# Flamingo block: the first layer's weight preparation moved into its attention, loads in pieces

## The reference

```python
x = x + tanh(g_xattn[0]) * L0_xattn(layernorm(x), ctx_1024, Wq, Wk, Wv, Wo, gq, gk)

q = (h @ Wq).reshape(B, Sq, H, D)
k = (ctx @ Wk).reshape(B, Skv, H, D)
v = (ctx @ Wv).reshape(B, Skv, H, D)
q, k = rmsnorm(q, gq), rmsnorm(k, gk)
attn = softmax(einsum("bqhd,bkhd->bhqk", q, k) / sqrt(D))
out = einsum("bhqk,bkhd->bqhd", attn, v).reshape(B, Sq, H * D)
return out @ Wo
```

## Time and profile before

| | us |
|---|---|
| median of three runs | 1361.18 |
| lowest and highest | 1357.79, 1362.24 |
| profiled execution | 1358.81 |
| its span, first to last instruction | 1357.0 |
| PE busy (share of the span) | 1271.7 (94%) |
| DVE, ACT, POOL busy | 903.0, 775.1, 435.9 |

### The profile page before, as it was taken

How to read it: one execution, slowest core, us unless ns; L and a number is a source line. 1 busy time by engine, 2 the same in 40 slices (tenths; PEclk the granted TensorE clock), 3 DMA queues, 4 the chain that set the end, 5 groups by cost and what they waited for, 6 DMA issues and landing times. The chain is left out here.

```text
span 1357.0 us, 23635 instructions
## 1 busy us (share of the span) xinstructions
PE 1271.7 (94%) x8163; PEld 1126.9 (83%) x8163; DVE 903.0 (67%) x2515; ACT 775.1 (57%) x2112; POOL 435.9 (32%) x420
## 2 busy tenths in 40 slices
PE   3799999999999969999999987999999999998998
PEld 3588888888888858888888875899898988887987
DVE  4688888888987657743433344667676677786867
ACT  3577777777777714322222255666666666545552
POOL 1365556654665523200000001222124242252430
PEclk8899999999999969999999998999999999999999
DMA  7000000000000400210000020000000003413435
GB/s 255 9 1 2 9 1 0 0 8 0 0 0 1 99 1 1 84 41 1 0 0 1 1 70 16 1 9 1 1 17 25 1 32 129 114 63 91 127 93 183
DMA packets 44237, 50.50 MB, mean 37 GB/s; under 512 B 14345, under 2 KB 36370, under 8 KB 43378
## 3 DMA queue, kind: packets, MB, share of 16 engines
q1 hardware_dynamic: 40354, 38.92, 9.7%
q0 software_dynamic: 3792, 10.40, 2.1%
HBM read 36.82 MB, written 12.49 MB: 36 GB/s over the span
## 5 line engine op out<-in xcount | busy, mean ns | idle before, releaser
L955 POOL TENSOR_TENSOR probs_a<-probs_a,rden_a 128x512 f32<-128x512 f32 x128 | 133.2, 1041 | 337.5 <-DVE rden_a L914 337.5
L98 PE MATMUL bank<-wvo_hi,pc_hi_a 128*128 128x256 f32 x512 | 154.0, 301 | 1.9 <-DVE pc_lo_a L921 1.9
L1321 ACT ACTIVATE act_g_f<-bank 128x512 f32<-128x512 f32 x64 | 38.2, 597 | 189.2 <-PE bank L100 189.2
L99 PE MATMUL bank<-wvo_lo,pc_hi_a 128*128 128x256 f32 x512 | 144.2, 282 | 0.0
L100 PE MATMUL bank<-wvo_hi,pc_lo_a 128*128 128x256 f32 x512 | 144.2, 282 | 0.0
L1378 DVE TENSOR_TENSOR hid_f<-act_g_f,bank 128x512 f32<-128x512 f32 x64 | 44.0, 688 | 143.3 <-ACT act_g_f L1321 143.3
L826 ACT ACTIVATE pc_hi_a<-bank 128x512 fp32r<-128x512 f32 x128 | 76.6, 598 | 107.3 <-PE bank L100 105.4
L917 DVE TENSOR_TENSOR pt_lo_a<-bank,pt_hi_a 128x512 fp32r<-128x512 f32 x128 | 87.8, 686 | 58.9 <-ACT pt_hi_a L823 58.3
L817 ACT ACTIVATE probs_a<-bank,nbias_a,q_r_a 128x128 f32<-128x128 f32 x256 | 114.4, 474 | 21.5 <-DVE nbias_a L908 21.5
L921 DVE TENSOR_TENSOR pc_lo_a<-bank,pc_hi_a 128x512 fp32r<-128x512 f32 x128 | 88.1, 688 | 45.3 <-ACT pc_hi_a L826 45.3
L98 PE MATMUL bank<-xt_hi_f,w_gu_hi_f 128*128 128x512 f32 (+1 forms) x256 | 102.0, 399 | 0.0
(11 more groups left out here) (304 smaller groups left out, 3989.9 us busy)
## 6 DMA issues: line engine op xcount, KB each, us to landing
xs_raw_f<-rows_in SPq DMA_DIRECT2D x39, 129.0 KB
q_raw_p<-in_L_xattn_Wq SPq DMA_DIRECT2D x4, 1024.0 KB, 8.5
y_tok_f<-rows_out SPq DMA_DIRECT2D x4, 1024.0 KB, 9.6
we_raw<-in_L_ffn_We_gate_up SPq DMA_DIRECT2D x2, 1408.0 KB, 10.8
o_raw_p<-in_L_xattn_Wo SPq DMA_DIRECT2D x1, 2048.0 KB, 10.2
x_sb<-in_x SPq DMA_DIRECT2D x4, 512.0 KB, 13.8
ctx_raw_a<-in_ctx SPq DMA_DIRECT2D x8, 256.0 KB, 2.8
o_early<-in_L_xattn_Wo SPq DMA_DIRECT2D x1, 2048.0 KB, 15.0
```

The lines of the kernel that those rows point to most:

```text
L98: nc.tensor.matmul(out, w[0], x[0], start=start, stop=False)
L99: nc.tensor.matmul(out, w[0], x[1], start=False, stop=False)
L955: nc.gpsimd.tensor_tensor(probs[:, i % 2, :, :], probs[:, i % 2, :, :], scale, ALU.mult).then_inc(sem("probs_scaled"), 1)
```

## The change

For layer 0 the preparation block is gone (what is left serves layer 1 only and is renamed `prepare_second`). Its work becomes steps of the attention's own order:

- SP issues context of group 0, then a quarter of Wk (256 KB), the tokens of group 0, a quarter of Wq (512 KB), the two gain vectors, the second quarters, Wv, Wo, the other quarters, the other tokens and the gates' vectors.
- WK and WQ split one quarter each: the high part on ACT, the low part on DVE for quarters 0 and 1, on POOL for 2 and 3. VT, VTc are the transposes of Wv and their copies; VO, VOc the products of two heads and their split. VT and VO take part in the ring of two banks.
- VT 0 and 1 lie ahead of Q0 in the start part, VT 2 and 3 behind the first scores. Two VO fills go into the start quad and into each of the quads 1, 2 and 3, behind Kc3 and KTc3 (in quad 3 behind Qq2 and KTc3). Quarter 2 of both weights is split in the start quad, quarter 3 in quad 1.
- K, Q and W wait for their pieces. The first group's four quads are written out (part "first"), and the loop runs over two groups in place of three. In the start part Qv2 and Qv3 wait for QT0 and QT1.
- The raw matrices now lie in the space of the low parts (Wk, Wq, Wo) and of `wvo_hi` (Wv and its transposes). The tanh of the gates and the product of the gains move to VOc7 and KN0.

```diff
-                    sp.dma_start(small[:, 0:2], a["g_xattn"].partition_broadcast(P)).then_inc(loaded_s, 16)
-                    sp.dma_start(small[:, 2:4], a["g_ffn"].partition_broadcast(P)).then_inc(loaded_s, 16)
-                    sp.dma_start(small[:, 4:5], a["L0_xattn_gq"].rearrange("(p a) -> p a", a=1)).then_inc(loaded_s, 16)
-                    sp.dma_start(small[:, 5:6], a["L0_xattn_gk"].rearrange("(p a) -> p a", a=1)).then_inc(loaded_s, 16)
-                    sp.dma_start(v_raw[:, :], Wv).then_inc(loaded_v, 16)
-                    sp.dma_start(o_raw[:, :, :], Wo.rearrange("(h d) e -> d h e", d=P)).then_inc(loaded_o, 16)
                 for k in range(KD):
                     sp.dma_start(q_raw[:, k, :], Wq[k * P:(k + 1) * P]).then_inc(loaded_q[k], 16)
-                if layer == 0:
-                    sp.dma_start(k_raw[:, :], Wk).then_inc(loaded_k, 16)
-                if layer == 0:
-                    for g in range(G):
-                        tokens = slice(g * GB, (g + 1) * GB)
-                        sp.dma_start(core.x[:, tokens, :], a["x"][tokens].rearrange("b s d -> s b d")).then_inc(core.x_loaded[g > 0], 16)
...
-                    pool.wait_ge(raw_hi, 2)
-                    nc.gpsimd.tensor_tensor(w["q"][1][:, 1, :], q_raw[:, 1, :], f32(w["q"][0][:, 1, :]), ALU.subtract)
...
-                        nc.scalar.activation(w["q"][0][:, k, :], q_raw[:, k, :], ACT.Copy).then_inc(raw_hi, 1)
...
-                    act.wait_ge(loaded_k, 16)
-                    nc.scalar.activation(w["k"][0][:, :], k_raw[:, :], ACT.Copy).then_inc(raw_hi, 1)
...
-                        nc.vector.tensor_tensor(w["q"][1][:, 0, :], q_raw[:, 0, :], f32(w["q"][0][:, 0, :]), ALU.subtract)
...
-                    dve.wait_ge(raw_hi, KD + 1)
-                    nc.vector.tensor_tensor(w["k"][1][:, :], k_raw[:, :], f32(w["k"][0][:, :]), ALU.subtract)
...
+    start = listed("""
+        WK0 CT0 CT1 LNA0 K0 Kc0 K1 Kc1 Kq0 LNB0 Kr0 K2 Kc2 Kq1 Kr1 K3 Kc3 Kq2 Kr2 WQ0 X0 X1 Kq3 Kr3 KN0 KH0 KH1 KH2 KH3 WK1 WQ1 VT0 VTc0 VT1 VTc1
+        Q0 Qv0 Qq0 Q1 Qv1 Qq1 Qr0 Qp0 Q2 QT0 QTc0 Qv2 Qq2 Qr1 Qp1 Q3 QT1 QTc1 Qv3 Qq3 Qr2 Qp2 QT2 QTc2 Qr3 Qp3 QT3 QTc3
+        KT0 KTc0 KT1 KTc1 KT2 KTc2 KT3 KTc3""")
+    start += [("S", 0, NQ), ("Sm", 0, NQ), ("CN", 0, pre)] + listed("VT2 VTc2 VT3 VTc3")
+    start += with_weights([s for s in quad_order(NQ) if s[0] not in ("W", "E")], {"Kc3": "VO0", "Tl0": "VOc0", "KTc3": "VO1", "QTc3": "VOc1", "Rp2": "WK2", "KH3": "WQ2"})
     body = [s for j in range(1, NQ + 1) for s in quad_order(j)]
+    first = with_weights(quad_order(1), {"Kc3": "VO2", "Tl0": "VOc2", "KTc3": "VO3", "QTc3": "VOc3", "Rp2": "WK3", "KH3": "WQ3"})
+    first += with_weights(quad_order(2), {"Kc3": "VO4", "Tl0": "VOc4", "KTc3": "VO5", "QTc3": "VOc5"}) + with_weights(quad_order(3), {"Qq2": "VO6", "Th2": "VOc6", "KTc3": "VO7", "QTc3": "VOc7"}) + quad_order(NQ)
...
+                for s in orders["first"]:
+                    emit("first", 0, *s)
+                with emit.engine.Fori(1, G - 1) as g:
...
+            if L == 0:
+                def columns(t):
+                    return slice(t * QH * P, (t + 1) * QH * P)
+                def tokens(m):
+                    own = slice(m * GB, (m + 1) * GB)
+                    sp.dma_start(core.x[:, own, :], a["x"][own].rearrange("b s d -> s b d")).then_inc(core.x_loaded[m > 0], 16)
+                def keys_of(t):
+                    sp.dma_start(w["k_raw"][:, columns(t)], a["L0_xattn_Wk"][:, columns(t)]).then_inc(sem(f"wk_loaded{t}"), 16)
+                def queries_of(t):
+                    sp.dma_start(w["q_raw"][:, :, columns(t)], a["L0_xattn_Wq"].rearrange("(k p) n -> p k n", p=P)[:, :, columns(t)]).then_inc(sem(f"wq_loaded{t}"), 16)
+                keys_of(0)
+                tokens(0)
+                queries_of(0)
+                sp.dma_start(small[:, 4:5], a["L0_xattn_gq"].rearrange("(p a) -> p a", a=1)).then_inc(sem("gains_loaded"), 16)
+                sp.dma_start(small[:, 5:6], a["L0_xattn_gk"].rearrange("(p a) -> p a", a=1)).then_inc(sem("gains_loaded"), 16)
+                keys_of(1)
+                queries_of(1)
+                sp.dma_start(w["v_raw"][:, :], a["L0_xattn_Wv"]).then_inc(sem("wv_loaded"), 16)
+                sp.dma_start(w["o_raw"][:, :, :], a["L0_xattn_Wo"].rearrange("(h d) e -> d h e", d=P)).then_inc(sem("wo_loaded"), 16)
+                for t in range(2, NQ):
+                    keys_of(t)
+                    queries_of(t)
+                for m in range(1, G):
+                    tokens(m)
+                sp.dma_start(small[:, 0:2], a["g_xattn"].partition_broadcast(P)).then_inc(sem("small_loaded"), 16)
+                sp.dma_start(small[:, 2:4], a["g_ffn"].partition_broadcast(P)).then_inc(sem("small_loaded"), 16)
...
+                elif name == "VT":
+                    if i == 0:
+                        pe.wait_ge(sem("wv_loaded"), 16)
+                    for a_ in range(4):
+                        last = nc.tensor.transpose(bank[:, a_ * P:(a_ + 1) * P], w["v_raw"][:, (4 * i + a_) * P:(4 * i + a_ + 1) * P], core.ident[:, :])
+                elif name == "VO":
+                    if i == 0:
+                        pe.wait_ge(sem("wo_loaded"), 16)
+                        pe.wait_ge(sem("vt_copied"), 4)
+                    for h in (2 * i, 2 * i + 1):
+                        last = nc.tensor.matmul(bank[:, h % 2 * D:(h % 2 + 1) * D], w["v_t"][:, h, :], w["o_raw"][:, h, :], start=True, stop=True)
...
+                        pe.wait_ge(sem("wk_split"), t + 1)
...
+                        if L == 0:
+                            pe.wait_ge(sem("wq_split"), (j + 1) % NQ + 1)
...
+                    if L == 0 and i % 2 == 0:
+                        pe.wait_ge(sem("vo_split"), (j - 1) * 2 + i // 2 + 1)
...
+                elif name == "WK":
+                    act.wait_ge(sem(f"wk_loaded{i}"), 16)
+                    cols = slice(i * QH * P, (i + 1) * QH * P)
+                    nc.scalar.activation(w["k"][0][:, cols], w["k_raw"][:, cols], ACT.Copy).then_inc(sem("wk_hi"), 1)
+                elif name == "WQ":
+                    act.wait_ge(sem(f"wq_loaded{i}"), 16)
+                    cols = slice(i * QH * P, (i + 1) * QH * P)
+                    nc.scalar.activation(w["q"][0][:, :, cols], w["q_raw"][:, :, cols], ACT.Copy).then_inc(sem("wq_hi"), 1)
+                elif name == "VTc":
+                    nc.scalar.activation(flat(w["v_t"][:, 4 * i:4 * i + 4, :]), bank[:, :], ACT.Copy).then_inc(sem("vt_copied"), 1)
+                elif name == "VOc":
+                    nc.scalar.activation(flat(w["vo"][0][:, 2 * i:2 * i + 2, :]), bank[:, :], ACT.Copy).then_inc(sem("vo_hi"), 1)
+                    if i == 7:
+                        act.wait_ge(sem("small_loaded"), 32)
+                        nc.scalar.activation(core.gates[:, :], small[:, 0:4], ACT.Tanh).then_inc(sem("gates_made"), 1)
...
+                elif name == "WK" and i < 2:
+                    dve.wait_ge(sem("wk_hi"), i + 1)
+                    cols = slice(i * QH * P, (i + 1) * QH * P)
+                    nc.vector.tensor_tensor(w["k"][1][:, cols], w["k_raw"][:, cols], f32(w["k"][0][:, cols]), ALU.subtract).then_inc(sem("wk_split"), 1)
+                elif name == "WQ" and i < 2:
+                    dve.wait_ge(sem("wq_hi"), i + 1)
+                    cols = slice(i * QH * P, (i + 1) * QH * P)
+                    nc.vector.tensor_tensor(w["q"][1][:, :, cols], w["q_raw"][:, :, cols], f32(w["q"][0][:, :, cols]), ALU.subtract).then_inc(sem("wq_split"), 1)
+                elif name == "VOc":
+                    dve.wait_ge(sem("vo_hi"), i + 1)
+                    hi, lo = (flat(v[:, 2 * i:2 * i + 2, :]) for v in w["vo"])
+                    nc.vector.tensor_tensor(lo, bank[:, :], f32(hi), ALU.subtract).then_inc(sem("vo_split"), 1)
                 elif name == "Qv":
+                    if part == "start" and i >= 2:
+                        dve.wait_ge(filled["QT"], i - 1)
...
+                    if part == "start":
+                        dve.wait_ge(sem("gains_loaded"), 32)
+                        nc.vector.scalar_tensor_tensor(out=w["gain"][:, :], in0=small[:, 4:5], scalar=float(P) ** 0.5, in1=small[:, 5:6],
+                                                       op0=ALU.mult, op1=ALU.mult).then_inc(sem("gain_made"), 1)
...
+                elif name == "WK" and i >= 2:
+                    pool.wait_ge(sem("wk_hi"), i + 1)
+                    cols = slice(i * QH * P, (i + 1) * QH * P)
+                    nc.gpsimd.tensor_tensor(w["k"][1][:, cols], w["k_raw"][:, cols], f32(w["k"][0][:, cols]), ALU.subtract).then_inc(sem("wk_split"), 1)
+                elif name == "WQ" and i >= 2:
+                    pool.wait_ge(sem("wq_hi"), i + 1)
+                    cols = slice(i * QH * P, (i + 1) * QH * P)
```

(34 more changed lines are left out.)

123 lines of the change are left out of this document (45 added, 78 removed).

## The result

| us | before | after |
|---|---|---|
| median of four runs | 1359.49 (1356.7 to 1362.24) | 1342.97 (1342.83 to 1344.09) |
| profiled execution | 1358.81 | 1344.09 |
| its span | 1357.0 | 1342.4 |

The ratio is 0.9887, with a 95% interval of 0.9871 to 0.9903. The forecast was 1344, with 1338 to 1352 around it.

The account below looks back on a forecast made before the run. TensorE (PE) was taken as saturated except for a hole in the first 68 us. Gain 26.7 less 10.6 added gives 16.1: 1342.7 from the profiled execution, 1345.1 from the median; forecast 1344, range 1338 to 1352.

Parts of the forecast that it names:

- A: From kernel start to the first score product: first scores at 33.0 us instead of 59.74, a gain of 26.7 (25.2 to 28.0).
- The loads: At the start: queues move 400 GB/s once full, so wk 0 lands at about 4.3 us and the tokens at 5.6.
- The clock: Ahead of the first scores: Q0 and Q1 may run on PE at 1.2 GHz, costing 0 to 2.4 us; half taken.
- The port: Ahead of the first Q copy: DVE's wq 1 low split may wait out POOL's k_r power, 0 or about 2.5 us; half taken.
- Qv's new wait: Ahead of the first scores: Qv2 waits for QT0's fill because its tile is reused, with Qr1 and Qv3 behind it.
- B: Behind the first scores: added work costs 10.6 us (7.9 to 14), with 7.9 of PE work as floor and stalls on top.
- The start quad: First quad behind the first scores: ACT decides, growth 3.2 us (1.75 to 5), besides 0.9 for VT2, VT3 and their transposes.
- the cover of 2.1 us: In quad 1: 2.1 us of slack before PE asks for Rp0, plus 0.9 from the next fill, just covers POOL's late powers.
- quad 2: Third quad behind the first scores: two output fills, growth 2.0 us (1.75 to 2.5).
- The cold engine: Rival, chance 0.1: PE stays at 1.2 GHz until the first scores, costing 6 or 7 us less 1.2 counted; result 1350.
- Late pieces: Rival, chance 0.06: at the start wk 0 or the tokens land 5 to 15 us late, so the gain becomes 12 to 20.
- The dense quads: Rival, chance 0.07: ACT and POOL late beyond the slack in start quad and quad 1, added cost 18 us, result 1352.

## Why the prediction was right

- **What bounds.** A hole at the start and a saturated PE behind it: right. 6.95 us more for 7.0 of added products is the sharpest test of it.
- **A, 26.7 forecast (25.2 to 28.0), 25.1 measured,** a hair outside its own range. Three terms were off. The loads: wk 0 was at hand at 5.1 and the tokens at 7.65, not 4.3 and 5.6. I had lined the loads up one behind the other at 400 GB/s, which puts 1 MB ahead of the tokens' landing; they landed when about 1.5 MB had moved, and wq 0, issued next, came at 9.3. DVE had other work until 7.1, so this cost some 0.8 at K0 and 0.9 at KN (18.57, forecast 17.65). The clock: 9 slow Q products (1.8 us) and 8 slow transposes (0.7 to 0.9), about 2.6, over the bound of 2.4, from which the transposes were missing. The port: nothing for the split, where up to 2.5 was bounded, and the step "waits out the POOL instruction under way" was wrong for the power. For clock and port together the sum held 1.2 (31.8 to 33.0), so the clock alone took 1.4 more than both had. With 0.8 from the loads that is 2.2, of which a chain 0.6 shorter than laid out gave some back: 1.64 us late (34.64 against 33.0). The clock's size is partly chance: other traces have fewer slow Q products.
- **Qv's new wait** showed for Qv3, as one DVE wait of 1.39 us for QT1. Q3's last product ended at 28.54 and Qv3 started at 29.01, so only some 0.5 us of it are new. From KT0 at 31.10 it was 3.54 us to the scores, where I took 3.8.
- **B, 10.6 forecast, 11.55 measured,** within 7.9 to 14. The start quad (4.1 against 3.96) and quads 1 and 3 were right. T0 in quad 1 waited for nothing, so the cover of 2.1 us over POOL's late powers held. The step that failed is quad 2, 3.28 where its range ended at 2.5: I had checked the fills against the ring at K, Q and QT and missed that CT1 in quad 2 alone takes the bank of VO5. The experiment with the earlier copy took 1.24 us of it away, and the 0.33 us of quad 4, which I had at nothing. The lengths named as signs for quads 2 and 3 (28.6 and 29.3) had too low a base: before, these quads took 27.35 and 27.82 us, so growth of 2.0 meant 29.4 and 29.8.
- **Rivals.** The cold engine up to the first scores didn't come (full clock from 23.6). Late pieces didn't come, but the run with the old order shows what that rival would have been worth: 16.1 us, the whole gain. The dense quads gave back 3.7 us beyond PE's floor of 7.9, far from the 10 of that rival.
- **Size.** The sum gave 16.1 us, and what it was a sum of, the attention, gained 13.6: A was 1.6 too high and B 1.0 too low. The changes of the profiled executions, 14.7, and of the medians, 16.5, lie closer to 16.1 only by stages that the sum didn't have, which move by several us from trace to trace. That the forecast of 1344 came within 1 us of the median is luck to that extent; the mechanism is right by the stages above.

## What to carry to other kernels

A preparation stage is worth dissolving if the first consumer's loads go first: here taking out the order of the loads cost 16 of 25 us and taking out the pieces 6 (the two don't add up, since each was taken out alone), and the missing barrier and the pieces with the old order paid for nothing but the work added behind the first scores. Work taken out of a stage with an idle engine and put behind it, where the same engine is saturated, is paid in full; look first for gaps ahead of the bottleneck, and for banks that are unused there, before spreading it. And when a fill is added to a shared ring, go through every later fill two places behind it, in those rounds too that hold a step which the others don't.

## What was not expected of the hardware

- Transposes held the full clock: in all three runs that had them ahead of Q the Q products started 0.23 us apart from the first pair on, and in all eight without added work three to nine started 0.43 us apart. Whether they would also raise it from half clock is open: in the three runs K had reached 0.23 before they began, and behind the v transposes of the earlier trace rows the products still came slowly.
- The granted clock reads 1.00 at the start whatever PE's speed: in the run with added products PE worked from 7.5 to 16.5 us, but for 0.8, with its products 0.43 us apart. In the run with the split behind the power the reading lasts longer still. Its Q products started 0.43 us apart from 20.36 to 23.77 us, beside a column that says 1.00 throughout. This is one stretch of it, in the view of the stages:

```profile
20.00:22.00 2.00, 2.00 (x5) 1.58 (x6) 0.93 (x1) 0.44 (x1) 2.00 (x1) 1.00 1.04 385
```

  With the loads in the old order a 1.00 stands even beside K products at 0.43 us up to 29.99. So a 1.00 at the start of these traces is no evidence unless equal products beside it start 0.23 us apart; the 0.50 ahead of the first scores came with the slow spacing wherever it was seen.
- A power of 128x16 on POOL (3.2 us) left a DVE split of two SBUF inputs at 1.24 us; a scaling of 128x512 stretched it to 1.97, and the next scaling, 2.02 in place of 1.04, waited for it. The wait is not for splits alone: in the change a DVE scaling of 128x4 took 0.65 us in place of 0.17 and ended at 26.24, with POOL's last k scaling (26.21). It cost at most 0.1 us, as Qv2 behind it (26.15) had to wait for QT0 until 26.06 anyway.
- The same order of loads had K0 start between 6.87 and 7.87 us in different executions.
